# Normalised rows made by ScalarE instead of VectorE in the six norm stages of a transformer kernel

## What is computed

```python
def _layernorm(x, axis=-1, eps=1e-05):
    m = jnp.mean(x, axis=axis, keepdims=True)
    v = jnp.var(x, axis=axis, keepdims=True)
    return (x - m) / jnp.sqrt(v + eps)
...
x = x + 0.5 * _L0_ffn_ref(_layernorm(x, axis=-1), ...)
x = x + _L0_attn_ref(_layernorm(x, axis=-1), ...)
x = x + 0.5 * _L0_ffn_ref(_layernorm(x, axis=-1), ...)
x = x + 0.5 * _L1_ffn_ref(_layernorm(x, axis=-1), ...)
x = x + _L1_attn_ref(_layernorm(x, axis=-1), ...)
x = x + 0.5 * _L1_ffn_ref(_layernorm(x, axis=-1), ...)
```

## Time and profile before

| stage | sublayer | combines | first norm starts, us | last norm starts, us | us between them |
|---|---|---|---|---|---|
| 1 | feed-forward, 2 experts | 0 | 7.37 | 21.04 | 13.67 |
| 2 | attention | 1 | 159.88 | 172.89 | 13.01 |
| 3 | feed-forward, 2 experts | 0 | 382.13 | 393.99 | 11.86 |
| 4 | feed-forward, 8 experts | 1 | 503.58 | 516.49 | 12.91 |
| 5 | mixer | 2 | 693.24 | 707.17 | 13.93 |
| 6 | feed-forward, 8 experts | 0 | 878.20 | 890.98 | 12.78 |

### The profile page before, as it was taken

How to read it: one execution, slowest core, us unless ns; L and a number is a source line. 1 busy time by engine, 2 the same in 40 slices (tenths; PEclk the granted TensorE clock), 3 DMA queues, 4 the chain that set the end, 5 groups by cost and what they waited for, 6 DMA issues and landing times.

```text
span 1063.4 us, 21229 instructions
## 1 busy us (share of the span) xinstructions
PE 844.0 (79%) x7724; PEld 545.1 (51%) x7725; DVE 610.2 (57%) x1153; ACT 351.7 (33%) x811; POOL 491.5 (46%) x538
## 2 busy tenths in 40 slices
PE   3089935888787667996869999868579978899995
PEld 1046622422232243664459999733324444699994
DVE  4723317486888252333636556468389855655654
ACT  2322201225565511221214544316601122354441
POOL 2218866128888321211225555122489742455531
PEclk9999987898899998999869999979999998899997
DMA  8213441425554910001666667240000001766644
GB/s 302 90 31 113 120 142 51 149 65 188 181 182 151 374 59 21 30 25 55 266 272 220 231 244 243 73 165 1 0 1 1 0 1 41 244 236 245 237 165 134
DMA packets 47751, 142.23 MB, mean 134 GB/s; under 512 B 10577, under 2 KB 23714, under 8 KB 41154
## 3 DMA queue, kind: packets, MB, share of 16 engines
q0 software_dynamic: 19280, 93.40, 26.3%
q1 hardware_dynamic: 22366, 40.92, 10.8%
q10 hardware_dynamic: 6036, 6.95, 1.9%
HBM read 106.11 MB, written 35.16 MB: 133 GB/s over the span
## 4 chain that ended last, share of the span: by engine, by line
PE 59%; DVE 16%; DMA 7%; ACT 7%; POOL 5%; issue 4%; SPq 1%; ACTq 0%; DVEq 0%; POOLq 0%
PE psum L553 15%; PE psum L526 12%; PE psum L512 7%; PE psum L1796 3%; DVE mem L1422 3%; ACT mem L1376 3%; DMA mem<-w2l_dram 2%; PE psum L114 2%; POOL mem L236 2%; PE psum L1309 2%; PE psum L1281 2%; PE psum L186 2%; PE psum L499 1%; PE psum L1823 1%; DVE mem L305 1%
## 5 line engine op out<-in xcount | busy, mean ns | idle before, releaser
L553 PE MATMUL psum<-mem 128*128 x1536 | 178.8, 273 | 3.6 <-DVE mem L791 2.4
L553 PEld LDWEIGHTS psum<-mem 128*128 128x128 f16 x1536 | 146.5, 98 | 23.5 <-issue 4.6
L902 POOL DMA_INDIRECT y_dram<-mem x64 | 63.5, 992 | 149.1 <-DVE mem L807 146.4
L526 PE MATMUL psum<-mem 128*128 128x128 f16 x2208 | 132.2, 220 | 0.0
L526 PEld LDWEIGHTS psum<-mem 128*128 128x128 f16 x2208 | 128.3, 99 | 0.7
L643 ACT ACTIVATE mem<-psum,mem 128x128 f32<-128x128 f32 x368 | 105.1, 369 | 54.0 <-PE psum L526 52.4
L897 POOL DMA_INDIRECT mem<-xn_dram,mem x64 | 65.0, 1016 | 116.1 <-PE psum L499 91.6
L1376 ACT ACTIVATE mem<-psum 128x512 f32<-128x512 f32 (+1 forms) x160 | 80.0, 552 | 81.1 <-PE psum L1289 61.6
L512 PE MATMUL psum<-mem 128*128 x432 | 102.8, 397 | 0.8 <-issue 0.8
L1422 DVE TENSOR_REDUCE mem<-psum 128x2 f32<-128x1024 f32 (+2 forms) x96 | 87.9, 950 | 25.7 <-PE psum L1263 15.1
L798 DVE CAST mem<-mem 128x512 f16<-128x512 f32 x92 | 45.6, 495 | 79.0 <-ACT mem L643 77.8
(11 more groups left out here) (248 smaller groups left out, 1463.3 us busy)
## 6 DMA issues: line engine op xcount, KB each, us to landing
stage<-in_w POOLq DMA_DIRECT2D x20, 480.0 KB, 4.6
stage<-in_w POOLq DMA_DIRECT2D x16, 512.0 KB, 3.9
w_rows<-mem SPq DMA_DIRECT2D x4, 2048.0 KB, 18.2
w2h_dram<-mem POOLq DMA_DIRECT2D x20, 240.0 KB, 2.8
w2l_dram<-mem POOLq DMA_DIRECT2D x20, 240.0 KB, 3.3
xn_dram<-mem ACTq DMA_DIRECT2D x32, 128.0 KB, 1.7
mem<-w2h_dram SPq DMA_DIRECT2D x2, 2048.0 KB, 14.0
mem<-w2l_dram SPq DMA_DIRECT2D x2, 2048.0 KB, 19.8
```

Of the source, the lines that this page charges most:

```text
L526: ins = eng.matmul(c.bank(2 * p + j // half)[:, j % half * P:(j % half + 1) * P], mats[q][:, l, k, j * P:(j + 1) * P], x[:, p, k, :], star ...
L553: ins = eng.matmul(c.bank(6)[:, 0:D], a[:, 0 if gated else p, q * half + j, :], w[:, at], start=(i == 0), stop=(i == 3 * CF - 1))
L902: eng.indirect_dma_start(c.y_dram[:, :], bass.IndirectOffsetOnAxis(ap=yidx[:, b:b + 1], axis=0), yo[:, b % 2, :], None).then_inc(s_ys[b % ...
```

## The change

The norm leaves VectorE. ScalarE makes it instead as scale * x + bias with a scale and a bias per token: the scale is `rstd`, the bias is -mean * rstd. ScalarE makes the bias itself in two small steps over 128x1: the negated mean (new L174) and its product with `rstd` (new L183). The norm is then L185. Three instructions a tile come onto ScalarE, in one queue with the high part and the store's DMA issue; one a tile leaves VectorE. A second edit gives one group of semaphores of the attention a shared name, which changes no instruction's order.

```diff
+    s_sh = c.sem("ln_shift", 2 * NT)
...
-            if 1 <= i <= NT:
-                t = order[i - 1]
-                eng.wait_ge(*s_rs(i))
-                eng.tensor_scalar(XN[:, t, :], X[:, t, :], mv[:, t, 0:1], rstd[:, t:t + 1],
-                                  ALU.subtract, ALU.mult).then_inc(s_xn.sem, 1)
...
     def act(eng):
-        for i in range(NT):
-            eng.wait_ge(*s_tps(i + 1))
-            eng.activation(XTh[:, :, tok(order[i])], pst(i), ACT.Copy).then_inc(s_hi.sem, 1)
-            if stored is not None:
-                stored(eng, order[i])
+        for i in range(NT + 1):
+            if i < NT:
+                t = order[i]
+                eng.wait_ge(*s_ag(i + 1))
+                eng.activation(shift[:, t, 0:1], mv[:, t, 0:1], ACT.Copy, scale=-1.0).then_inc(s_sh.sem, 1)
+            if i:
+                eng.wait_ge(*s_tps(i))
+                eng.activation(XTh[:, :, tok(order[i - 1])], pst(i - 1), ACT.Copy).then_inc(s_hi.sem, 1)
+                if stored is not None:
+                    stored(eng, order[i - 1])
+            if i < NT:
+                eng.wait_ge(*s_sh(2 * i + 1))
+                eng.wait_ge(*s_rs(i + 1))
+                eng.activation(shift[:, t, 1:2], shift[:, t, 0:1], ACT.Identity, scale=rstd[:, t:t + 1]).then_inc(s_sh.sem, 1)
+                eng.wait_ge(*s_sh(2 * i + 2))
+                eng.activation(XN[:, t, :], X[:, t, :], ACT.Identity, bias=shift[:, t, 1:2], scale=rstd[:, t:t + 1])\
+                    .then_inc(s_xn.sem, 1)
...
-    s_ld = [n(f"ld{i}", 16 * 4 * ((PAIRS + STACKS - 1 - i) // STACKS)) for i in range(STACKS)]
+    s_ld = [c.sem(f"tile_in{i}", 16 * 4 * ((PAIRS + STACKS - 1 - i) // STACKS)) for i in range(STACKS)]
```

More of the change, by code:

```diff
@@ L134, in layernorm_stage @@
     X, XTh, XTl = c.X, c.XTh, c.XTl
-    stats, mv, rstd = c.ln_stats, c.ln_mv, c.ln_rstd
+    stats, mv, rstd, shift = c.ln_stats, c.ln_mv, c.ln_rstd, c.ln_shift
     order, ready, combine = src["order"], src["ready"], src["combine"]
@@ L2169, in program @@
         c.ln_rstd = c.sb("ln_rstd", [P, NT], F32)
+        c.ln_shift = c.sb("ln_shift", [P, NT, 2], F32)
         c.ln_consts = c.sb("ln_consts", [P, 2], F32)
```

## The result

The changed kernel takes 1076.05 us (median of 20 runs, 1071.67 to 1089.69). The kernel before, measured beside it, takes 1070.28 us (20 runs, 1059.34 to 1080.27). The ratio is 1.0084, with a 95% interval of 1.0061 to 1.0107: some 9 us slower, with an interval that just reaches beyond 1%. The medians of all runs lie 5.8 us apart. The forecast was +6.2 us, or 0.58%. It matches the medians and lies just under the interval of the ratio. The profiled execution after has a span of 1071.4 us, against 1063.4 before, with nearly the same mean granted clock (0.933 and 0.935 of full speed).

The account below looks back on a forecast made before the run. The prediction took norm stages to be bound by a ring of latency that no engine fills. Stages 1, 3 and 6 +5.2, stage 2 +0.5, stage 4 +0.5, stage 5 0 made +6.2 on 1071.22: 1077.4 us, range 1068 to 1086.

Parts of the forecast that it names:

- the ring: Norm stages, norm to next norm: 1.69 us a tile becomes 1.86 with a store, 1.75 without; 2.11 and 2.00 at 1.2 GHz.
- Rival B: ScalarE steps in the norm stages are cheap, per-partition operands costing nothing: 1068.5 us; chance 0.09.
- The step from the high part to the product: ScalarE's queue, from start of high part to product: 0.38 to 0.39 us with a store's DMA issue between, 0.28 without.
- Rival C: ScalarE's queue is serial, each step waiting for the last and the DMA issue paid in full: 1086 us; chance 0.11.
- The first norm: Start of each norm stage, waiting for rstd: 0.34 for the product and 0.19 for the longer norm, 0.53 us once.
- Stage 2: Norm stage 2: first norm and slower tiles +0.9, last norm no longer slowed beside GpSimd's cast -0.4; together +0.5 us.
- Stage 4: Norm stage 4 to its last combine: +0.53 start, +0.4 four tiles (rstd's two-tile ring 1.87 each), -0.46 earlier combine; +0.5 us.
- Stages 1, 3 and 6: Norm stages with store and no combine: 0.53 + 7 x 0.17 = 1.72 us each, 5.2 together.
- Rival D: Longer gaps leave TensorE at 1.2 GHz for more tiles, 0.25 us each: 1081 to 1082 us; sign 0.69 transposes; chance 0.10.
- Stage 5: Norm stage 5 to its last second combine: what the ring loses, VectorE's shorter queue gives back; 0 us.
- Rival A: VectorE's time makes a norm stage, so 48 norms taken off save 16.3 us: 1055 us; could hold in stage 5; chance 0.03.
- Rival E: No effect, 1071 us, because the norm stages' exits hang on other work; only stages 4 and 5 show such cover; chance 0.05.

Follow-up runs that it names:

- double product: The changed kernel with the product mean * rstd made twice in a row on ScalarE; 1.0215 times the kernel before.
- the product on GpSimd: The changed kernel with the product mean * rstd made by GpSimd right after rstd instead of ScalarE; 0.9984 times the kernel before.
- the norm ahead: The kernel before with VectorE's order changed alone, norm ahead of the previous tile's low part: 0.9758. On ScalarE, the changed kernel so reordered, product on GpSimd: 0.9857.
- the store behind the norm: The changed kernel with the store's DMA issue moved behind the next norm on ScalarE; 1.0027, then 1.0018 times the kernel before.
- the fourth filler: The changed kernel with four filler matmuls a tile instead of three; 1.0027 times the kernel before.
- stage 5 only: The kernel before with the change in norm stage 5 alone, and the semaphore name; 1.0007 times the kernel before.

## Why the prediction was right, and where its terms were off

The mechanism was right, and the measured time lies in the stated range. The sum was short: the stages grew by 8.0 us and not by 6.2. The prediction also took 1% as the least that runs of this kernel can tell; the interval came out at 0.23% each way.

**What bounds the stage.** Right. The stages are rings of latency closed by the order of a queue. The double product (a step more, paid in full in stage 1), the product on GpSimd (a step less, the loss gone) and the norm ahead (the ring open, 2.4% faster with the same instructions on the same engines) are three tests of this with three signs.

**The ScalarE durations.** Right. The norm takes 0.60 us (forecast 0.593) and the product 0.29 (0.296), in the groups by line:

```profile
L183 ACT ACTIVATE ln_shift<-ln_shift,ln_rstd x48: 285/294/296, 7.4 to 898.6; 128x1 f32<-128x1 f32 x48
...
L174 ACT ACTIVATE ln_shift<-ln_mv x48: 185/188/205, 6.4 to 897.5; 128x1 f32<-128x1 f32 x48
```

(ns, least, median and most of 48.) The negation takes 0.19 and is hidden in the wait for the transposes, as said. Rival B is out by this alone. The Trainium skill, "ScalarE: Activation LUTs", "What ACT_TABLE_LOAD costs", gives 186 ns and 0.833 ns an element, with 93 ns for each per-partition operand. By that the norm would take an estimated 0.585 and the product 0.280; the trace has 0.60 and 0.294, so the page agrees within 5%.

**The step from the high part to the product.** This is the term that was mis-sized. I had 0.39 with a store, from one row in which an instruction began 0.04 after the end of a DMA issue. Measured are 0.44 to 0.46: the product starts 0.10 after the end of the issue's row. Without the issue it is 0.28, as forecast (the store behind the norm). The ring is 1.89 at 2.4 GHz and 2.14 at 1.2 GHz, not 1.86 and 2.11. The row had a table load behind a long issue, not an operation with data behind a short one, and I took it for one. In the kernel before two table loads also stand right behind a store's issue of 0.33, and they start 0.07 after its end. What makes up the rest, the kind of operation or its two waits, is not shown. Over 21 tiles the ring's 0.03 are 0.6 us. Rival C had the right place but not the size: it would have made the step 0.76, and it is 0.45.

**The first norm.** It was to cost 0.53. In stages 1, 3 and 6, which have no combine, it cost 0.58. In stages 2 and 4 it cost 0.84 and 0.83, and here the prediction missed a step. The timeline of stage 4 after the change:

```profile
509.25 0.47 DVE L869 SCALAR_TENSOR_TENSOR X<-mem,X 128x256 f32<-128x256 f32 x1
509.31 0.83 POOL L164 TENSOR_TENSOR ln_rstd<-ln_rstd,ln_consts 128x1 f32<-128x1 f32 x1
...
510.24 0.29 ACT L183 ACTIVATE ln_shift<-ln_shift,ln_rstd 128x1 f32<-128x1 f32 x1 [1.04 <-POOL ln_rstd L164]
```

And the same place in the kernel before:

```profile
502.98 0.57 POOL L168 TENSOR_TENSOR ln_rstd<-ln_rstd,ln_consts 128x1 f32<-128x1 f32 x1
503.58 0.41 DVE L160 TENSOR_SCALAR mem<-X,ln_mv,ln_rstd 128x256 f32<-128x256 f32 x1 [0.59 <-POOL ln_rstd L168]
503.91 0.48 DVE L861 SCALAR_TENSOR_TENSOR X<-mem,X 128x256 f32<-128x256 f32 x1
```

Before, VectorE stood still while GpSimd made the first rstd, because its norm waited for it, and the third combine came after. With the norm gone nothing holds the combine, so it runs beside the power, and the power takes 0.83 instead of 0.57. Stage 2 shows 0.84 against 0.57. A wait that seemed to cost VectorE something had kept the road clear for GpSimd.

The traces of all the runs bear this out. In 20 places a combine was already running when a power started, and there the power took 0.83 or 0.84 us every time. Where neither a combine nor a VectorE norm ran beside it, over 500 times, it took 0.55 to 0.57; stages 1, 3 and 6 of the changed kernel, which have no combine, are among these. What matters is that the combine starts first. In stage 5 of the changed kernel it starts 0.24 us after the power, and the power is not stretched:

```profile
699.50 0.57 POOL L164 TENSOR_TENSOR ln_rstd<-ln_rstd,ln_consts 128x1 f32<-128x1 f32 x1
699.74 0.47 DVE L869 SCALAR_TENSOR_TENSOR X<-mem,X 128x256 f32<-128x256 f32 x1
```

So the engines do not meet only at semaphores, as the first section has it. How they meet, the runs do not show. The Trainium skill, "SBUF — State Buffer", "SBUF: two separate sides", has a port pair that VectorE and GpSimd lock against each other, the first to start for its whole instruction, also for a VectorE operation with two inputs in SBUF, as the combine is. The trace agrees in direction, and in that the operation that starts first is not held up. By a full block until the combine's end the power would take up to 0.41 longer (509.31 to 509.72); measured are 0.26. And the combine that starts second in stage 5 takes 0.47 as elsewhere, where a full block would hold it up.

**Stage 2.** +0.93 against +0.5. First norm 0.84 (0.53 forecast). The seven periods cost 0.53 (13.01 us before, 13.54 after) against 0.36. The last norm beside GpSimd's cast took 0.60 and not more, as forecast, so the stretch behind it shrank. That part was right: ScalarE is not disturbed there, and VectorE was the earlier trace rows. The timeline after:

```profile
173.76 1.04 POOL L266 CAST mem<-stage 128x1024 f16<-128x1024 f32 x1
...
174.63 0.60 ACT L185 ACTIVATE mem<-X,ln_shift,ln_rstd 128x256 f32<-128x256 f32 x1
```

In the last periods the step from rstd to the product is what is waited for, as the prediction said:

```profile
172.57 0.30 ACT L183 ACTIVATE ln_shift<-ln_shift,ln_rstd 128x1 f32<-128x1 f32 x1 [0.20 <-POOL ln_rstd L164]
```

Rstd is late at every second tile and the norms come 2.04 and 1.73 apart, 1.88 in the mean, where the forecast was 1.87.

**Stage 4.** +0.91 against +0.5. To the first low part it is +0.83 (0.53 forecast, the power again), the four tiles to the fifth low part +0.54 (0.4), and the combine comes 0.46 earlier behind its low part, as forecast. I had expected rstd's ring at 1.87; the ring through the store, 1.89, is the longer one.

**Stages 1, 3 and 6.** 6.0 against 5.2 in the sum. Seven periods cost 0.20 each and not 0.17. Stage 3 stands out with +2.73 and stage 6 with +1.29, because stage 3 has three more tiles at 1.2 GHz and stage 6 three fewer. That the two cancel is luck. Behind stage 1 the profile before has 3, 0, 2, 3 and 4 such tiles in stages 2 to 6, and the profile after 3, 3, 2, 2 and 1. TensorE's timeline in stage 3 after shows the drop behind the first tile:

```profile
386.75 0.44 PE L194 MATMUL psum<-ident,mem 128*128 128x128 f32 x2 [3.33 <-ACT mem L185]
388.67 0.69 PE L194 MATMUL psum<-ident,mem 128*128 128x128 f32 x2 [0.83 <-ACT mem L185]
390.81 0.69 PE L194 MATMUL psum<-ident,mem 128*128 128x128 f32 x2 [0.17 <-ACT mem L185]
```

**Rival D** read from stage 3 alone would look confirmed, 0.69 where 0.44 had stood: that was the sign that the prediction named for it. Over the kernel its price did not show: 12 slow tiles before, 11 or 12 after, and the fourth filler did not bring stage 3's back. In part the places of these tiles shift on their own. The kernel with only the semaphore renamed had 3, 0, 2, 2 and 1, so stage 6 went from four to one with no change in its norm stages, and the second profile of the changed kernel had 2, 2, 3, 2 and 1. But stage 3 is steady in one thing: it had no slow tile in the four profiles whose ring is 1.69 or less with three fillers (before, the name alone, stage 5 only, the product on GpSimd), and one to three in the five with a longer ring but a single product. Against that, the two kernels with the norm ahead and three fillers, whose tiles are the shortest, had four. So whether the change brought the slow tiles to stage 3 stays open. Over the whole kernel the counts behind stage 1 are 8 to 12 in the three profiles with the norm of before in stages 1 to 4 and 6, and 10 to 14 in those five, so a tile or two may be the change's, and 0.5 us with them. With the ring at 2.2 (the double product) there were 26, in one profile, so longer gaps do go with the lower clock once they are long enough. A stage's difference has to be cleared of such tiles (0.25 us each) before it is compared with a ring.

**Stage 5.** +0.18 against 0, and the experiment gives +0.20. **Rival A** is refuted there and everywhere else.

**Rival E** held only where the prediction had it. In stages 4 and 5, 0.8 and 0.6 us of the longer stage come behind the last combine. The chain of waits after the change still goes from the last combine of stage 4 over SyncE's loads to TensorE at 549.2, so they are covered there. The stretches that follow are 1.2 and 0.8 shorter than before, which fits, but they vary too much between profiles to show it.

**The sum.** The forecast of 6.2 lacked 0.8 in stages 1, 3 and 6, 0.4 each in stages 2 and 4, and 0.2 in stage 5. That makes 8.0, which lies between the 5.8 of the medians and the 9 of the ratio.

## What to carry to other kernels

Before work is moved to a less busy engine, walk once round the loop that one tile makes and ask what the next tile's first instruction stands behind in its queue. If that loop is longer than any engine's work in it, the shares of busy time do not decide: the move is worth the difference of two latencies, while a change of order that breaks the loop was worth 2.4% here with no work moved. An instruction that waits may also keep an engine quiet for a neighbour, so ask what runs in its place when it is gone.

## What the runs showed of the hardware that was not expected

- A DMA issue in ScalarE's queue holds back the product behind it for longer than its row: 0.33 us for the row, then 0.10 until the product starts, in all 28 tiles with a store. Beside the high part the net price is 0.17 a tile.
- GpSimd's power over 128x1 takes 0.55 to 0.57 us alone and 0.83 to 0.84 when a VectorE combine was already running at its start. In the kernel with the norm ahead on VectorE its median is 0.62: beside the norm it takes 0.62 to 0.69 in 26 of 48 tiles, and 0.83 or 0.84 beside the combine in two.
- The long stretches between the norm stages differ from one execution to another with the same instructions. From stage 2 to stage 3 they took 205.5 us before, 207.6 and 203.4 in two profiles of the changed kernel, and 208.6 in the kernel with only the semaphore renamed, and from stage 4 to 5 172.9, 171.7 and 181.1. One pair of spans cannot price a change of this size; the lengths of the stages it touches can.
